# Interleaving the first normalisation's projections with the fold of the edge sums in a two-layer graph network kernel

## The chip, the cores and the metric

One core of a Trainium2 chip runs the whole kernel. The metric is device time in microseconds (us), the median of three runs. Engines are named as in the profile: PE (TensorE; PEld are its weight loads), DVE (VectorE), ACT (ScalarE), POOL (GpSimd), and SP, which issues DMAs.

## The reference

12500 nodes with 64 features, 400000 edges sorted by target, 64 features per edge. Two graph layers, each followed by a residual and a normalisation over the 64 features:

```python
def _L0_gnn_ref(x, src, dst, W_fc, b_fc, W_res, b_res):
    agg = segment_sum(x[src], dst, n)
    deg = segment_sum(ones_like(dst), dst, n)
    mean = agg / maximum(deg, 1.0)[:, None]
    h = relu(concatenate([x, mean], axis=-1) @ W_fc + b_fc)
    return h + x @ W_res + b_res

def _general_conv(x, edge_attr, src, dst, Wm, bm, We, be, Ws, bs):
    msg = x[src] @ Wm + bm + edge_attr @ We + be
    return segment_sum(msg, dst, n) + x @ Ws + bs

x = _layernorm(x + _L0_gnn_ref(x, ...))
x = _layernorm(x + conv2(relu(conv1(x))))      # both use edge_attr
```

## The kernel before, in words

The nodes lie in 98 blocks of 128 (`BLOCKS`). There are three rounds (`for r in range(3)`), and each adds up the rows of neighbours for one layer. Round 0 also builds a matrix of edge counts, and after its own sums it walks over all edge features: 728 edge steps (`ESTEPS`), eight at a time in a loop (`EB`), in which DVE marks targets (L931), ACT widens the marks (L1440), PE multiplies (L1196, one of eight PSUM banks per step) and DVE adds a finished bank to `sums_e` (L944; the last six banks, L955). `sums_e` lies over the whole of `abuf`, the buffer of the counts. SP loads the edge features (L1561), eight steps ahead.

Each block of `sums_e` holds two halves that must be added and turned. That is the fold: PE multiplies every block by `twofold`, two identities on top of each other (L1205, 98 blocks in 13 groups of up to 8, `FOLDS`, PSUM banks 0 to 3), and ACT copies each group into `easf`, which lies in `early` (L1445, counted by `e_out`).

Then comes the first normalisation, in 14 iterations of 7 blocks (`NITER`, `NB`):

- SP loads a piece of x, turned (L1525, 224 KB, two buffers `turned_a`, whose last row is set to one at L737).
- PE multiplies its 7 blocks by `w_in`, which holds `W_fc` and `W_res` with the biases in a 65th row (L1086, banks 4 and 5 or 6 and 7; `a_prod`). Iteration i waits until DVE has read the banks of iteration i-2 (`a_relu`). A float32 product shows as two instructions, so 7 blocks are 14 rows.
- POOL scales the neighbour sums by `rdeg`, the reciprocal of the degree (L1257).
- DVE adds (L743), takes the relu and adds the residual (L745), sums the squares of the iteration before (L749, which waits for ACT's squares, L1363), sums for the mean (L752) and subtracts it (L754). A square root on ACT (L1365) and a reciprocal on DVE (L757) follow the last iteration.

A second loop of 14 iterations then scales (L768), turns (L1047) and projects (L1104) the rows for round 1.

All buffers of the normalisation lie in `abuf`, over `sums_e`. So every engine waits for `round_done`, which DVE raises (L960) when the last group of the fold is copied. `rdeg` is computed just before that (L957, L958). The order of all engines is written by hand; each engine runs its own program in order and meets the others through semaphores, and SP's DMAs go out in the order of its program.

## Time and profile before

| | |
|---|---|
| median of three runs | 3532.28 us (3532.06 to 3535.52) |
| profiled execution: its time | 3533.11 us |
| profiled execution: its span, first to last instruction | 3531.3 us |
| busy share of the span | PE 88%, PEld 81%, DVE 68%, POOL 60%, ACT 45% |
| mean granted TensorE clock | 0.963 of full speed |
| last add of the edge sums (L955) starts | 1979.78 us |
| fold on PE (L1205) | 1980.12 to 2002.2 us |
| projections on PE (L1086) | 2006.22 to 2052.6 us |
| reciprocal after the first normalisation (L757) starts | 2058.09 us |

The page has a share of busy time for the whole span, but the change touches 80 us of it, from the last edge steps near 1975 us to the second loop at 2059 us. So what matters is read from views of that stretch: the chain of waits, the table by stretches with the granted clock, and the groups of instructions.

### The profile page before, as it was taken

The numbers are of one execution on the slowest core, as the hardware profiler recorded it, in microseconds if no ns is written. First come the engines' busy times: TensorE is split into PE (matmuls) and PEld (weight loads), VectorE is DVE, ScalarE is ACT, GpSimd is POOL, SyncE is SP. The second block draws the span as 40 slices with busy tenths as digits, with TensorE's granted clock in tenths as the row PEclk, the third lists the DMA queues.
The fourth block names the chain that finished last, engine by engine and source line by source line (L and its number), as shares of the span: only waits on it lengthen the run. The fifth ranks groups of instructions, "written<-read, shape, count | busy, mean of one in ns | idle before, by whom it ended". The sixth has DMA issues, their size and how long they took to land.

```text
span 3531.3 us, 114817 instructions
## 1 busy us (share of the span) xinstructions
PE 3093.6 (88%) x38568; PEld 2874.1 (81%) x38568; DVE 2388.2 (68%) x6286; ACT 1585.1 (45%) x2164; POOL 2120.9 (60%) x2436
## 2 busy tenths in 40 slices
PE   0128999999999999899999979999999889999995
PEld 0127988888888888788888879999999789999995
DVE  8679998888888888799999673333333433333335
ACT  0122677778999999789999550000000400000000
POOL 5771345455666666544444257777777777777774
PEclk9859999999999999999999879999999999999998
DMA  3521455556666666678888439999999499999995
GB/s 87 144 19 44 163 196 208 202 211 229 239 244 243 244 242 243 233 229 253 253 253 252 119 139 384 393 396 381 400 384 384 172 363 394 393 387 398 386 388 222
DMA packets 234014, 928.09 MB, mean 263 GB/s; under 512 B 46723, under 2 KB 146193, under 8 KB 178030
## 3 DMA queue, kind: packets, MB, share of 16 engines
q1 hardware_dynamic: 182405, 844.73, 63.8%
q0 software_dynamic: 51392, 80.97, 7.9%
q10 hardware_dynamic: 154, 1.60, 0.2%
q8 instruction: 34, 0.56, 0.1%
q14 instruction: 29, 0.24, 0.0%
HBM read 676.56 MB, written 250.56 MB: 263 GB/s over the span
## 4 chain that ended last, share of the span: by engine, by line
PE 40%; POOL 19%; issue 17%; DVE 14%; DMA 5%; DVEq 5%; ACT 1%; ACTq 0%; POOLq 0%; SPq 0%
PE ps L1126 27%; POOL msg L1288 13%; PE ps L1149 8%; DVE union L816 5%; DMA msg<-y_tab,idx 3%; POOL abuf L1230 3%; DVE union L931 3%; PE ps L1118 3%; DVE abuf L944 3%; DVEq L944 2%; DVEq L471 2%; POOL union L1230 1%; PE ps L1086 1%; DMA abuf<-in_x_dram 1%; PE ps L1205 1%
## 5 line engine op out<-in xcount | busy, mean ns | idle before, releaser
L1288 POOL DMA_INDIRECT msg<-y_tab,idx x1512 | 1611.3, 1066 | 922.2 <-issue 469.6
L1126 PE MATMUL ps<-union,abuf 128*128 128x192 bf16 x14112 | 1206.4, 248 | 14.9 <-DVEq L787 10.2
L1126 PEld LDWEIGHTS ps<-union,abuf 128*128 128x128 f16 x14112 | 1173.6, 99 | 17.9 <-issue 10.6
L1418 ACT ACTIVATE abuf<-ps 128x784 f16<-128x784 f32 x1152 | 949.1, 824 | 261.4 <-PE ps L1149 236.6
L816 DVE TENSOR_TENSOR union<-lane,union 128x1568 f16<-128x1568 f16 (+1 forms) x1384 | 911.7, 710 | 8.5 <-PE ps L1149 4.6
L1126 PE MATMUL ps<-early,abuf 128*128 128x195 bf16 x7154 | 809.3, 249 | 0.0
L1126 PEld LDWEIGHTS ps<-early,abuf 128*128 128x128 f16 x7154 | 641.9, 99 | 92.1
L1149 PE MATMUL ps<-union 128*128 128x98 f16 (+2 forms) x4192 | 661.8, 287 | 56.7 <-DVE union L816 55.5
L1394 ACT ACTIVATE idx<-src_g 128x7 int32 (+1 forms) x216 | 44.4, 205 | 1257.1 <-PE ps L1118 1237.9
L808 DVE TENSOR_TENSOR acc<-acc,ps 128x64 f32 (+1 forms) x1015 | 225.0, 222 | 412.4 <-DVE acc L808 239.3
L1196 PE MATMUL ps<-union 128*64 128x128 f32 x7280 | 458.7, 278 | 24.0 <-ACT union L1440 19.6
L1196 PEld LDWEIGHTS ps<-union 128*64 128x64 f32 x7280 | 395.5, 137 | 87.4 <-DVE abuf L944 74.3
L1440 ACT ACTIVATE union<-union 128x1280 f32<-128x1280 f16 x364 | 443.5, 1268 | 35.8 <-DVE union L931 35.3
L1149 PEld LDWEIGHTS ps<-union 128*128 128x128 f16 x4192 | 353.7, 108 | 98.5 <-issue 59.3
L1308 POOL TENSOR_TENSOR rel_e<-early,base_e 128x10 f16 x728 | 226.1, 330 | 247.4 <-DVE union L931 244.5
L931 DVE TENSOR_TENSOR union<-lane,rel_e 128x640 f16<-128x640 f16 x728 | 352.2, 484 | 4.4 <-POOL rel_e L1308 1.4
L895 DVE TENSOR_REDUCE part_d<-ps 128x64 f32<-128x192 f32 x144 | 51.6, 358 | 353.1 <-PE ps L1126 353.1
L794 DVE TENSOR_SCALAR hot_g<-lane,codes 128x128 f16<-128x128 f16 x1008 | 184.2, 269 | 63.9 <-DVE acc L808 62.2
L1118 PE MATMUL ps<-msg,hot_g 128*128 128x64 bf16 (+1 forms) x4536 | 181.7, 195 | 45.8 <-DMA msg<-y_tab,idx 45.3
L944 DVE TENSOR_TENSOR abuf<-abuf,ps 128x128 f32 x728 | 204.9, 281 | 15.8 <-issue 7.2
L1118 PEld LDWEIGHTS ps<-msg,hot_g 128*128 128x128 f16 x4536 | 169.1, 99 | 54.4 <-DMA msg<-y_tab,idx 53.8
L865 DVE TENSOR_TENSOR acc<-acc,ps 128x65 f32 x504 | 110.0, 218 | 69.0 <-DVE acc L865 53.8
(229 smaller groups left out, 1342.2 us busy)
## 6 DMA issues: line engine op xcount, KB each, us to landing
abuf<-a_dram SPq DMA_DIRECT2D x288, 1568.0 KB
a_dram<-abuf SPq DMA_DIRECT2D x72, 3136.0 KB
union<-in_edge_attr_dram SPq DMA_DIRECT2D x728, 160.0 KB, 3.1
msg<-y_tab,idx POOLq DMA_INDIRECT x1512
y_tab<-union SPq DMA_DIRECT2D x28, 336.0 KB, 2.2
abuf<-in_x_dram SPq DMA_DIRECT2D x28, 224.0 KB, 3.5
y_tab<-early SPq DMA_DIRECT2D x7, 682.5 KB, 5.2
out_dram<-union SPq DMA_DIRECT2D x2, 800.0 KB, 3.5
```

Source lines behind the costliest of these rows:

```text
L808: V.tensor_tensor(to, to, tile_ps(r, j, k).unsqueeze(1), ALU.add).then_inc(s_add[r], 1)
L816: return V.tensor_tensor(to.rearrange("p s (c u) -> p s c u", u=2), lanes.unsqueeze(1).to_broadcast([P, n, width // 2, 2]), codes[:, which ...
L931: marks = V.tensor_tensor(mark_e[:, h, :, :].rearrange("p j (c u) -> p j c u", u=2), lane16[:, 0:P].rearrange("p (c u) -> p c u", u=2).uns ...
L944: V.tensor_tensor(to, to, ps[:, b, 0:P], ALU.add).then_inc(e_add, 1)
L1118: last = nc.tensor.matmul(tile_ps(r, j, k), hot_g[:, s, :], msg[:, s, c * width_of[r]:(c + 1) * width_of[r]], start=c == 0, stop=c == 2)
L1126: last = nc.tensor.matmul(ps[:, bank, 0:3 * width_of[r]], abuf[:, buffer, hi * P:(hi + 1) * P], ycols[r][:, hi, :], start=hi == 0, stop=hi ...
L1149: nc.tensor.matmul(ps[:, w % 4, 0:WIN].rearrange("p (h d) -> p h d", d=WD)[:, :, d0:d0 + wd], hot_c[:, n, WIN:WIN + P], hot_c[:, n, 0:HIS ...
L1196: last = nc.tensor.matmul(ps[half:half + D, h, 0:P], feats[:, h, j * D:(j + 1) * D], hot_e[:, h, j, :], start=j < 2, stop=j >= EG - 2)
L1288: pool.indirect_dma_start(msg[:, s, 0:3 * width_of[r]], None, y_tab[r], bass.IndirectOffsetOnAxis(ap=idx[:, s:s + 1], axis=0)).then_inc(ga ...
L1308: nc.gpsimd.tensor_tensor(rel_e[:, h, :, :], flat(dst_e[:, bass.ds(grp[h], 1), :]).unsqueeze(2) .to_broadcast([P, EG, 2]), base_e[:, bass. ...
L1418: A.activation(abuf[:, j, :].rearrange("p (h w d) -> p w h d", w=WPB, d=WD) [:, w:w + 2, :, :], ps[:, w % 4:w % 4 + 2, 0:WIN].rearrange("p ...
L1440: A.activation(hot_e[:, h:h + 2, :, :], mark_e[:, h:h + 2, :, :], ACT.Copy)\
```

## The change

The fold and the projections become one sequence on PE: projections 0 and 1, then by turns a group of the fold and a projection, each projection two ahead of the group. To make that possible, the normalisation's buffers leave `abuf`: `turned_a` goes to `early`, behind the fold's output, and `scaled_a`, `sum_a` and `square_a` go to the end of `union`, behind the buffers of the edge steps. `rdeg` and the rows of ones are made before the edge steps. SP loads x as soon as its last edge load is issued. POOL scales without waiting for `round_done`. ACT copies a group of the fold ahead of each square. `round_done` is raised after the reciprocal, ahead of the second loop.

```diff
@@ buffers
-        turned_a = norm_tile(XT, F1)
-        scaled_a, sum_a, square_a = (per_block(norm_tile(U)) for _ in range(3))
+        turned_a = [early[0:F1, BLOCKS * D + k * XT:BLOCKS * D + (k + 1) * XT] for k in range(2)]
+        BEHIND = EB * EG * (D + P // 2 + P)
+        scaled_a, sum_a, square_a = (per_block([union[:, BEHIND + (2 * n + k) * U:BEHIND + (2 * n + k + 1) * U]
+                                                for k in range(2)]) for n in range(3))
@@ DVE
-                    for t in turned_a:
-                        V.memset(t[D:F1, :], 1.0).then_inc(s_ones, 1)
...
                     dve.wait_ge(a_rstd, 1)
+                    dve.wait_ge(e_out, FOLDS)
+                    dve.sem_inc(round_done, 1)
...
+                for t in turned_a:
+                    V.memset(t[D:F1, :], 1.0).then_inc(s_ones, 1)
+                step(V.tensor_scalar(rdeg[:, :], acc[:, :, D], 1.0, None, ALU.max))
+                step(V.reciprocal(rdeg[:, :], rdeg[:, :]), "rdeg")
                 dve.wait_ge(s_pc, 1 + 2 * BC + BE)
...
-                dve.wait_ge(e_add, ESTEPS + LAG + EB)
-                step(V.tensor_scalar(rdeg[:, :], acc[:, :, D], 1.0, None, ALU.max))
-                step(V.reciprocal(rdeg[:, :], rdeg[:, :]))
-                dve.wait_ge(e_out, FOLDS)
-                dve.sem_inc(round_done, 1)
@@ PE
-                if r == 1:
-                    for i in range(NITER):
-                        pe.wait_ge(n_in[i % 2], 16 * (i // 2 + 1))
...
+                    def project(i):
+                        pe.wait_ge(n_in[i % 2], 16 * (i // 2 + 1))
+                        if i >= 2:
+                            pe.wait_ge(a_relu, i - 1)
+                        for b in range(NB):
+                            last = nc.tensor.matmul(both(i % 2, b), turned_a[i % 2][:, b * P:(b + 1) * P],
+                                                    w_in[:, :, :].rearrange("f c d -> f (c d)"), start=True, stop=True)
+                        last.then_inc(a_prod, 1)
+
+                    pe.wait_ge(s_ones, 2)
+                    pe.wait_ge(e_add, ESTEPS + 6 - (EB - LAG) + EB)
+                    project(0)
                     pe.wait_ge(e_add, ESTEPS + LAG + EB)
-                    for n in range(FOLDS):
...
+                    project(1)
+                    for n in range(NITER):
+                        if n < FOLDS:
+                            if n >= 4:
+                                pe.wait_ge(e_out, n - 3)
+                            for c in range(min(FB, BLOCKS - n * FB)):
+                                last = nc.tensor.matmul(ps[:, n % 4, c * D:(c + 1) * D], sums_e[:, n * FB + c, :],
+                                                        twofold[:, :], start=True, stop=True)
+                            last.then_inc(e_fold, 1)
+                        if n + 2 < NITER:
+                            project(n + 2)
@@ POOL
-                if r:
-                    pool.wait_ge(round_done, r + 1)
                 if r == 1:
+                    pool.wait_ge(s_v, mark["rdeg"])
                     for i in range(NITER):
...
+                if r:
+                    pool.wait_ge(round_done, r + 1)
@@ ACT
                     for i in range(NITER):
+                        if i < FOLDS:
+                            act.wait_ge(e_fold, i + 1)
+                            width = min(FB, BLOCKS - i * FB) * D
+                            A.activation(easf[:, i * FB * D:i * FB * D + width], ps[:, i % 4, 0:width], ACT.Copy)\
+                                .then_inc(e_out, 1)
                         act.wait_ge(a_mid, i + 1)
...
                     A.activation(rstd, root, ACT.Sqrt, bias=epst[:, :], scale=1.0 / D).then_inc(a_root, 1)
+                    act.wait_ge(round_done, r + 1)
...
-                    for n in range(FOLDS):
-                        act.wait_ge(e_fold, n + 1)
...
@@ SP
-                if r:
-                    sp.wait_ge(round_done, r + 1)
-                else:
+                if r == 0:
                     sp.wait_ge(s_v, mark["prepared"])
...
                         sp.dma_start(turned_a[i % 2][0:D, :], x[:, i * XT:(i + 1) * XT]).then_inc(n_in[i % 2], 16)
+                if r:
+                    sp.wait_ge(round_done, r + 1)
```

PE's program behind the loop of edge steps, before (L1196 edge steps, L1205 fold, L1086 projections, L1047 the second loop's turning; a float32 product counts once here):

```order
L1196 MATMUL ps<-union 64x128 x5
L1189 REGISTER_ALU
L1189 COMPARE_AND_BRANCH
L1205 MATMUL ps<-twofold,abuf 128x64 x98
L1086 MATMUL ps<-w_in,abuf 128x128 x98
L1047 MATMUL ps<-ident,abuf 128x128 x14
```

and now (L1186 edge steps, L1195 projections, L1209 fold):

```order
L1186 MATMUL ps<-union 64x128 x5
L1179 REGISTER_ALU
L1179 COMPARE_AND_BRANCH
L1195 MATMUL ps<-w_in,early 128x128 x14
L1209 MATMUL ps<-twofold,abuf 128x64 x8
L1195 MATMUL ps<-w_in,early 128x128 x7
L1209 MATMUL ps<-twofold,abuf 128x64 x8
L1195 MATMUL ps<-w_in,early 128x128 x7
```

Two projections lead, and from then on each group of 8 blocks of the fold is followed by one projection of 7 blocks; all 98 and 98 blocks are still there.

ACT's program in the same place, before (L1440 edge steps, L1445 copies of the fold, L1363 squares):

```order
L1440 ACTIVATE union<-union 128x1280 x4
L1435 REGISTER_ALU
L1435 COMPARE_AND_BRANCH
L1445 ACTIVATE early<-ps 128x512 x12
L1445 ACTIVATE early<-ps 128x128
L1363 ACTIVATE abuf<-acc 128x448 x14
L1365 ACT_TABLE_LOAD
```

and now (L1370 copies, L1375 squares):

```order
L1453 ACTIVATE union<-union 128x1280 x4
L1448 REGISTER_ALU
L1448 COMPARE_AND_BRANCH
L1370 ACTIVATE early<-ps 128x512
L1375 ACTIVATE union<-acc 128x448
L1370 ACTIVATE early<-ps 128x512
L1375 ACTIVATE union<-acc 128x448
```

The square of iteration i, for which DVE's next iteration waits, now stands behind the copy of fold group i.

## Rows read from the trace of the kernel before

**Rows 1.** Chain of waits, edge steps to second loop (start us, us, what).

```profile
1979.78 0.30 DVE abuf L955
1980.12 21.67 PE ps L1205 x192
...
2002.65 3.44 DMA abuf<-in_x_dram
2006.22 3.34 PE ps L1086 x14
2009.58 3.25 DMA abuf<-in_x_dram
...
2049.76 0.63 DVE abuf L743
...
2052.77 0.63 DVE abuf L743
```

**Rows 2.** Table by stretches (stretch, length, busy by engine, PEclk, DMA share, GB/s).

```profile
core 0: us, PE busy (x) PEld busy (x) DVE busy (x) ACT busy (x) POOL busy (x), PEclk, DMA share, GB/s
1980.10:2002.20 22.10, 22.08 (x196) 21.96 (x196) 1.01 (x2) 6.96 (x12) 0.00 (x0) 1.00 0.01 1
2002.20:2006.20 4.00, 0.02 (x1) 0.01 (x1) 1.61 (x2) 0.38 (x2) 1.83 (x2) 0.89 0.44 115
2006.20:2012.50 6.30, 6.28 (x28) 6.04 (x28) 2.49 (x4) 0.16 (x1) 0.94 (x1) 0.50 0.14 36
2006.20:2052.60 46.40, 45.11 (x196) 42.63 (x196) 37.34 (x64) 6.92 (x12) 15.58 (x16) 0.50 0.21 60
...
2059.50:2062.90 3.40, 3.33 (x16) 3.33 (x17) 0.61 (x3) 1.54 (x3) 0.00 (x0) 0.50 0.92 295
2064.00:2068.00 4.00, 3.97 (x37) 3.78 (x36) 2.06 (x4) 3.71 (x9) 1.39 (x2) 1.00 0.11 44
```

**Rows 3.** Timeline of PEld (start us, us, engine, line, operation, count).

```profile
2019.47 3.06 PEld L1086 LDWEIGHTS ps<-w_in,abuf 65*128 65x128 f32 x14 [0.56 <-DMA abuf<-in_x_dram]
2059.57 2.85 PEld L1047 LDWEIGHTS ps<-ident,abuf 128*128 128x128 f32 x14 [7.20 <-DVE abuf L768]
...
2073.73 0.75 PEld L1047 LDWEIGHTS ps<-ident,abuf 128*128 128x128 f32 x7 [0.53 <-DVE abuf L768]
2074.45 1.64 PEld L1104 LDWEIGHTS ps<-w_cat,abuf 128*128 128x128 f32 x14
```

**Rows 4.** Timeline of the hand-over from edge steps to fold.

```profile
1971.72 2.55 SPq L1561 DMA_DIRECT2D union<-in_edge_attr_dram  x4
1977.58 1.08 PEld L1196 LDWEIGHTS ps<-union 128*64 128x64 f32 x20 [0.26 <-issue]
1978.56 0.29 DVE L955 TENSOR_TENSOR abuf<-abuf,ps 128x128 f32 x1 [0.26 <-DVE abuf L955]
```

**Rows 5.** Groups of instructions from 1980 to 2059 us.

```profile
L1257 POOL TENSOR_TENSOR abuf<-acc,rdeg 128x448 f32<-128x448 f32 x14 | 13.1, 937 | 63.1 <-DVE abuf L743 32.0 <-DVEq L960 31.0
L743 DVE TENSOR_TENSOR abuf<-abuf,ps 128x448 f32<-128x448 f32 x14 | 8.7, 620 | 9.7 <-PE ps L1086 9.6
L1363 ACT ACTIVATE abuf<-acc 128x448 f32<-128x448 f32 x14 | 8.1, 577 | 45.7 <-DVE acc L754 45.7
L1445 ACT ACTIVATE early<-ps 128x512 f32<-128x512 f32 (+1 forms) x13 | 7.3, 572 | 17.9 <-PE ps L1205 17.9
L737 DVE MEMSET abuf<- 1x896 f32 x2 | 1.6, 805 | 21.9 <-ACT early L1445 21.8
L958 DVE RECIPROCAL rdeg<-rdeg 128x98 f32<-128x98 f32 x1 | 0.8, 766 | 0.0
```

**Rows 6.** DMA issues from 1980 to 2059 us (KB each, median us to landing).

```profile
abuf<-in_x_dram SPq DMA_DIRECT2D x14, 224.0 KB, 3.3
```

**Rows 7.** Timeline ahead of the edge steps.

```profile
1492.88 5.33 POOL L1302 MEMSET abuf<- 128x6272 f32 x1 [19.16 <-DVEq L913]
1498.07 0.23 DVE L918 TENSOR_TENSOR twofold<-ident 128x64 f32<-128x64 f32 x1 [7.47 <-ACT early L1339]
```

More of the change, by code:

```diff
@@ L326, in gnn_program @@
         bias_b = per_block(norm_tile(U))
-        turned_a = norm_tile(XT, F1)
         assert used[0] <= HIS * P // 2
-        used[0] = 0
-        scaled_a, sum_a, square_a = (per_block(norm_tile(U)) for _ in range(3))
-        assert used[0] <= HIS * P // 4
+        turned_a = [early[0:F1, BLOCKS * D + k * XT:BLOCKS * D + (k + 1) * XT] for k in range(2)]
+        BEHIND = EB * EG * (D + P // 2 + P)
+        scaled_a, sum_a, square_a = (per_block([union[:, BEHIND + (2 * n + k) * U:BEHIND + (2 * n + k + 1) * U]
+                                                for k in range(2)]) for n in range(3))
+        assert BLOCKS * D + 2 * XT <= YW0 and EG * GROUPS <= BLOCKS * D and BEHIND + 6 * U <= UNION
+        assert FOLDS <= NITER
         regs = smallf[:, 11 * CG:11 * CG + 64]
@@ L1076, in _ @@
                     pe.wait_ge(round_done, r + 1)
-                    pe.wait_ge(s_ones, 2 * min(r, 1))
                 pe.wait_ge(s_v, mark["prepared"])
-                if r == 1:
-                    for i in range(NITER):
-                        pe.wait_ge(n_in[i % 2], 16 * (i // 2 + 1))
-                        if i >= 2:
-                            pe.wait_ge(a_relu, i - 1)
-                        for b in range(NB):
-                            last = nc.tensor.matmul(both(i % 2, b), turned_a[i % 2][:, b * P:(b + 1) * P],
-                                                    w_in[:, :, :].rearrange("f c d -> f (c d)"), start=True, stop=True)
-                        last.then_inc(a_prod, 1)
                 for i in range(NITER + 1) if r else ():
@@ L1198, in _ @@
                             last.then_inc(e_mm[h], 1)
-                    pe.wait_ge(e_add, ESTEPS + LAG + EB)
-                    for n in range(FOLDS):
-                        if n >= 4:
-                            pe.wait_ge(e_out, n - 3)
-                        for c in range(min(FB, BLOCKS - n * FB)):
-                            last = nc.tensor.matmul(ps[:, n % 4, c * D:(c + 1) * D], sums_e[:, n * FB + c, :], twofold[:, :],
-                                                    start=True, stop=True)
-                        last.then_inc(e_fold, 1)
+                    def project(i):
[9 more added lines that the diff above has]
+                    project(0)
+                    pe.wait_ge(e_add, ESTEPS + LAG + EB)
+                    project(1)
[9 more added lines that the diff above has]
+                            project(n + 2)
         @block.gpsimd
@@ L1352, in _ @@
             for r in range(3):
-                if r:
+                if r == 2:
                     act.wait_ge(round_done, r + 1)
-                else:
+                elif r == 0:
                     act.wait_ge(s_v, mark["prepared"])
@@ L1441, in _ @@
                                 .then_inc(e_hot[h // 2], 1)
-                    for n in range(FOLDS):
-                        act.wait_ge(e_fold, n + 1)
-                        width = min(FB, BLOCKS - n * FB) * D
-                        A.activation(easf[:, n * FB * D:n * FB * D + width], ps[:, n % 4, 0:width], ACT.Copy)\
-                            .then_inc(e_out, 1)
             squares = union[:, 0:BLOCKS * D].rearrange("p (b d) -> p b d", d=D)
@@ L1515, in _ @@
             for r in range(3):
-                if r:
-                    sp.wait_ge(round_done, r + 1)
-                else:
+                if r == 0:
                     sp.wait_ge(s_v, mark["prepared"])
```

## The prediction

> **What bounds the kernel now.** I read the chain of waits first, where the last link of each step stands. From the last add of the edge sums to the second loop it is one thread: the fold on PE (21.67 us), a wait for x (3.44), and then by turns a pair of projections on PE (about 3.35 us a projection) and a wait of about 3.3 us for the next piece of x, up to DVE's last two iterations, which start at 2049.76 and 2052.77 [rows 1]. Nothing runs beside the fold but ACT's copies.
>
> Then I read the table by stretches, for the clock. Here the reader is to see something that the busy shares hide: PE is granted 1.00 (2.4 GHz) all through the fold; it idles while x is on its way, and the clock has fallen by 2006.2; and the projections then run at 0.50 (1.2 GHz) for 46 us, although PE is busy in 45.1 of 46.4 us [rows 2]. So the projections are slow for two reasons: a 3.3 us load that two buffers do not hide, and half the clock. Third, the timeline of weight loads gives the price of the same work at both levels: 14 loads of a projection (7 blocks) take 3.06 us at half clock; the second loop's projections, as many columns but 128 rows instead of 65, take 1.64 us for 14 at full clock [rows 3].
>
> **The change, part by part.**
>
> *Where PE starts.* The fold waits for the last add of the edge sums; projection 0 needs only the banks 4 and 5, whose adds are done with the fourth of the six last ones, 1978.56 + 0.29 = 1978.85. PE's last edge step issues its loads until 1978.66 [rows 4]. So projection 0 starts at about 1978.95, and the wait for the last add (1980.07) ends inside it. For this x must be there. SP is done with the edge loads at 1971.72 + 2.55 = 1974.27 [rows 4], and x took 3.44 us the first time, two loads together, and 3.3 after that [rows 1, 6]: it lands near 1978, with no edge load behind it on the queue. 0.9 us of slack; if it is late, PE waits that much once.
>
> *The sequence on PE.* 14 projections and 12 full groups of the fold stand ahead of the end of projection 13 (the thirteenth group, 2 blocks, comes after it). A group is 16 of the 196 instructions that took 22.1 us, 1.80 us [rows 2], 12 of them 21.6. For a projection I have two ends: 3.06 us at half clock and 1.64 at full [rows 3]. I take 1.64, 14 of them 22.96, because the fold alone held 1.00 for 22 us [rows 2], the edge steps ahead of it run at full clock too, and PE now goes from the one to the other without the idle stretch in which the clock fell. PE ends projection 13 at 1978.95 + 22.96 + 21.6 = 2023.5.
>
> *No new wait inside it.* Projection i+2 needs its x, issued when projection i ends; between them lie two groups and a projection, 1.80 + 1.64 + 1.80 = 5.24 us, against 3.3 us to landing [rows 6]. Only projection 2 has less, 1.64 + 1.80 = 3.44 us; the load of x is about 0.1 us faster. The relu of iteration i, for which projection i+2 waits, comes 1.3 us after DVE starts on it and has as much room. POOL's scaling (0.94 us each [rows 5]) starts as soon as POOL's part of the edge steps ends and is never last.
>
> *DVE and ACT.* DVE needs 3.01 us an iteration (2049.76 to 2052.77 [rows 1]), less than PE's 1.64 + 1.80 = 3.44. But ACT now copies fold group i ahead of square i, and DVE's iteration i+1 waits for that square. From the end of projection i+1: the group 1.80, copy 0.57, square 0.58 [rows 5], then DVE's last three operations, 3.01 less two of 0.62 and their gaps, 1.74, and some 0.15 of hand-overs: 4.84 us. That is 1.4 us after the next projection ends. It does not add up over iterations, since neither the group nor the projection waits for this end, only for the relu in front of it. So DVE starts its last iteration 1.4 us behind PE, at 2024.9. Before, it started at 2052.77. What follows (the last iteration, the root, the reciprocal) is the same work: **27.9 us gained**.
>
> *What is moved.* The rows of ones (1.6 us) and the reciprocal of the degrees (0.77 and a shorter operation [rows 5]) go ahead of the edge steps, into 7.47 us in which DVE waited for ACT's copies of the targets [rows 7]: nothing, while that cover is there; without it 2.6 us. POOL clears half of `sums_e` beside them, as before, until 1498.2, right behind that cover.
>
> *Behind the loop.* `round_done` now comes after the reciprocal, and behind it ACT's first copy of the second loop, POOL's biases and SP's loads. ACT's copy ran 0.9 us earlier before, but PE also needs DVE's scaled rows, which end as late; POOL's first bias is due some 7 us after. I take nothing, at most 0.1. PE idles some 7 us ahead of the second loop, as before (2052.6 to 2059.57), and starts it at half clock in both. There, 14 loads take 2.85 us where 7 take 0.75 at full [rows 3]: between a start at full clock and as long again at half, 1.35 us either way. I take nothing.
>
> *Sum.* 3533.11 us is the profiled execution, 0.83 above the median of 3532.28; against the latter **3504.4 us**. A run of this kernel tells a change from none at about 0.2%, 7 us.
>
> **A rule against the rows.** The clock fell while PE idled, and did not come back under projections that kept PE busy; other work did bring it back: the second loop starts at 0.50 and has 1.00 from 2064 [rows 2]. The Trainium skill (TensorE: Matmul & The Clock Gate, section "Why this matters for your kernels") says that matmuls keep the fast clock as long as PE does not idle between bursts. By that rule the new sequence stays at full clock and 3504.4 stands; by the same rule the projections of before should have risen, and the row says 0.50, so here page and measurement differ, and the measurement decides. The trace has no projection at full clock. That leaves rivals 1 and 2.
>
> **The rivals.**
>
> 1. *The projections pull the clock down, and the fold with it: slower.* For it: 46 us of them at 0.50 with PE busy [rows 2]. Against it: they were never at full clock to begin with, and half the time now goes to work that held it. Price: a weight load of 128 rows took 2.85/14 at half and 0.75/7 at full, 1.90 times as long [rows 3], so a group 3.42 us; 1978.95 + 14 x 3.06 + 12 x 3.42 = 2062.8, DVE 0.2 behind: 10.2 us later than before, 3542.5 us. It is slower than before from a group of 2.57 us on.
> 2. *Half clock in the projections, full in the fold*, or half in part of the stretch: 1978.95 + 14 x 3.06 + 12 x 1.80 = 2043.4, DVE 0.2 behind, 9.2 us gained: 3523.1.
> 3. *The chain over ACT sets the pace.* Should the 4.84 us (group, copy, square, DVE's end) come in series, because PE falls behind DVE after all, DVE's last iteration starts at 1980.8 + 13 x 4.84 = 2043.7: 3523.2. Against it: PE waits for the relu alone.
> 4. *x comes late every time.* If it takes 6.6 us, twice the 3.3 [rows 6], two projections go by in 6.6 + 1.64 us, 4.12 instead of 3.44 each, 8.2 us over 12: 3512.6. Against it: the DMA queues carry nothing else there.
> 5. *The order on PE is not what sets the end*, say because ACT's copies hold the banks: no change. The chain speaks against it.
>
> **How the numbers follow.** Forecast 0.76, rival 1 0.08, rival 2 0.07, rivals 3 and 4 0.04 each, rival 5 0.01. The forecast's own ends: 1.4 us less if DVE keeps up, 1.35 less if the second loop starts at full clock, some 0.8 less if projections of 65 rows go a little faster than 1.64; the other way the same, and 2.6 if the moved operations are not covered: 3500 to 3511. To hold 8 in 10 the range goes on to rivals 2 to 4: 3500 to 3524. Faster by over 0.2% is the forecast and rivals 2 to 4, 0.90; within 0.2% 0.02; slower, rival 1, 0.08.
>
> **What would show it.** In the table by stretches of the changed kernel: PEclk 1.00 from 1979 to 2023, where 0.50 in any part of it is rival 1 or 2. In the chain: PE's projections and fold by turns without a DMA between them, and DVE's last iteration at 2024.9. In the timeline: 14 weight loads of a projection in 1.64 us, groups of 1.80, projection 0 at 1979. In the groups: DVE's L749 waiting for ACT's square, some 0.4 us each time. DVE's moved operations between 1490.6 and 1493.5 with L918's counterpart where it was. Wrong is the forecast if a projection takes 3 us, if PE waits for x, or if the stretch up to the edge steps grows.

## The result, and the profile after

The changed kernel takes 3510.43 us (median of 4 runs, 3509.63 to 3512.45) against 3533.90 us for the kernel before in the same comparison (4 runs, 3532.06 to 3536.56). The ratio is 0.9934, with a 95% interval of 0.9918 to 0.9949: 23.5 us faster, where 27.9 were forecast. The profiled run took 3509.63 us with a span of 3507.9 us, and the mean granted clock of the whole span went from 0.963 to 0.970.

The stage itself went as forecast. The chain of waits of the changed kernel, from the first projection on (start us, us, what; L1195 projections, L1209 fold, L743 the first operation of an iteration on DVE, its last start the last iteration):

```profile
1985.37 1.81 PE ps L1195 x14
1987.18 0.02 issue
1987.20 3.27 DMA early<-in_x_dram
1990.47 0.04 issue
1990.51 1.83 PE ps L1195 x14
1992.34 1.73 PE ps L1209 x16
1994.07 1.62 PE ps L1195 x14
...
2025.84 1.75 PE ps L1209 x16
...
2028.11 0.58 ACT union L1375
2028.71 0.62 DVE small L749
...
2030.43 0.62 DVE union L743
```

Before, the chain passed through a DMA between the projections [rows 1]. Now x is on the chain only once, and from 1990.5 on a projection (1.62 us) and a group of the fold (1.73) follow each other without a gap. The last link is the one over ACT that the prediction named: copy, square, DVE's sum of squares. The table by stretches shows why a projection takes 1.62 us:

```profile
core 0: us, PE busy (x) PEld busy (x) DVE busy (x) ACT busy (x) POOL busy (x), PEclk, DMA share, GB/s
1986.50:2027.60 41.10, 41.05 (x368) 40.91 (x368) 35.08 (x60) 11.68 (x22) 11.23 (x12) 1.00 0.25 68
```

PE is busy in 41.05 of 41.10 us, and the clock is 1.00 (2.4 GHz) in all of them, where the projections ran at 0.50 before [rows 2]. The weight loads, the wait of the prediction's projection 2 (0.18 us) and DVE's wait for the square, in the timeline and in the groups:

```profile
1985.34 3.20 PEld L1195 LDWEIGHTS ps<-w_in,early 65*128 65x128 f32 x28 [0.30 <-issue]
1988.46 1.87 PEld L1209 LDWEIGHTS ps<-twofold,abuf 128*128 128x128 f32 x16
1990.51 1.64 PEld L1195 LDWEIGHTS ps<-w_in,early 65*128 65x128 f32 x14 [0.18 <-DMA early<-in_x_dram]
```

```profile
L749 DVE TENSOR_REDUCE small<-union 128x7 f32<-128x448 f32 x14 | 8.7, 620 | 5.4 <-ACT union L1375 5.4
```

14 loads of 65 rows take 1.64 us [rows 3 have 3.06 at half clock], and a pair of projection and group 1.62 + 1.73 = 3.35 us in the chain. DVE's last iteration starts at 2030.43, 44.2 us after the last add of the edge sums (1986.20). Before it was 2052.77 less 1979.78, 73.0 us [rows 1]. So the stage gave **28.8 us**.

But the last add itself came at 1986.20 instead of 1979.78: **6.4 us of the gain were lost ahead of the stage**, in work that the prediction put down at nothing. Three points of the trace divide it: up to the start of the conversion of the edge targets (L886, before L884) the run was 1.05 us shorter; from there to the first marking of targets it took 14.1 us instead of 12.7; and from the first to the last of the 728 markings 480.1 instead of 474.1. Three sets of rows tell where. First the timeline ahead of the edge steps of the changed kernel:

```profile
1492.23 5.33 POOL L1309 MEMSET abuf<- 128x6272 f32 x1 [19.55 <-DVEq L915]
1492.47 1.75 DVE L920 MEMSET early<- 1x896 f32 x2 [2.93 <-issue]
1494.25 3.37 DVE L921 TENSOR_SCALAR rdeg<-acc 128x98 f32<-128x98 f32 x1
1497.66 0.77 DVE L922 RECIPROCAL rdeg<-rdeg 128x98 f32<-128x98 f32 x1
1498.46 0.22 DVE L924 TENSOR_TENSOR twofold<-ident 128x64 f32<-128x64 f32 x1
```

The shorter operation of `rdeg` (L921) takes 3.37 us, where it took 0.25 behind the loop in the kernel before. It ends at 1497.62, just after POOL's clearing of `sums_e` ends (1492.23 + 5.33 = 1497.56). The rows of ones (L920), beside the same clearing, take what they took, 0.805 us each [rows 5]. In all five traces with this order (the changed kernel twice, and three of the experiments below) L921 takes 3.36 or 3.37 us and ends 0.06 or 0.07 us after the clearing. The Trainium skill (SBUF — State Buffer, section "Who interferes with whom") says that a DVE `tensor_scalar` may use the ports that DVE shares with GpSimd, and that whichever of the two starts second is blocked until the other ends; the trace agrees, 3.37 us beside POOL and 0.25 without it.

Second, the end of the edge loop (L937 marks targets, L1262 is POOL's scaling):

```profile
1976.81 2.08 POOL L1262 TENSOR_TENSOR union<-acc,rdeg 128x448 f32<-128x448 f32 x2
1976.82 1.27 DVE L937 TENSOR_TENSOR union<-lane,rel_e 128x640 f16<-128x640 f16 x1
...
1978.21 1.02 DVE L937 TENSOR_TENSOR union<-lane,rel_e 128x640 f16<-128x640 f16 x1
...
1979.36 0.48 DVE L937 TENSOR_TENSOR union<-lane,rel_e 128x640 f16<-128x640 f16 x1
```

POOL's first two scalings no longer wait for the fold, so they run while DVE still marks, and two markings take 1.27 and 1.02 us instead of 0.48. From the 721st marking to the last it is 5.80 us in all five traces in which POOL scales this early, and 4.56 or 4.57 in the nine others: 1.24 us lost. The same section says that a DVE operation with both inputs in SBUF contends with a GpSimd operation that reads SBUF; a marking (`lane` and `rel_e`) is one, and the rows agree.

Third, the middle of the edge loop, where nothing was changed. The stretch from 1520 to 1960 us in both kernels, markings alone (L931 before, L937 now):

```profile
1520.00:1960.00 440.00, 328.27 (x679) 1.00 0.84 253
```

```profile
1520.00:1960.00 440.00, 325.83 (x671) 1.00 0.84 250
```

679 markings in 440 us before, 671 now, at the same clock. 32 steps, one turn of the loop, take 21.0 us instead of 20.75: from the 65th marking to the 721st it is 430.7 us instead of 425.6, 5.1 of the 6.0. A distance between two markings is 0.60 us, and 0.72 to 0.75 at every fourth (0.99 at the jump back), where DVE loads four block numbers into registers, which the trace doesn't count as busy. In the changed kernel two of the eight such places, the one 4 and the one 24 steps behind the jump back, take 0.87 and 0.86 us. DVE's program in front of the loop has become longer by the four moved operations.

### The profile page after: what moved, and what is told of

The parts are those of the page before. It is cut to its first block, busy times and chain, and to the rows that moved or that the text cites. A ratio compares the mean times of both kernels' runs of the same rounds, so it can differ in the third digit from the quotient of the medians.

```text
span 3507.9 us, 114818 instructions
## 1 busy us (share of the span) xinstructions
PE 3071.3 (88%) x38568; PEld 2853.7 (81%) x38568; DVE 2393.0 (68%) x6286; ACT 1584.9 (45%) x2164; POOL 2121.4 (60%) x2436
## 4 chain that ended last, share of the span: by engine, by line
PE 44%; POOL 17%; issue 15%; DVE 14%; DMA 5%; DVEq 5%; ACT 0%; ACTq 0%; POOLq 0%; SPq 0%
PE ps L1116 31%; POOL msg L1295 11%; PE ps L1139 8%; DVE union L818 5%; DMA msg<-y_tab,idx 4%; DVE union L937 3%; POOL abuf L1236 3%; PE ps L1108 3%; DVE abuf L950 2%; DVEq L950 2%; DVEq L473 2%; POOL union L1236 1%; PE ps L1195 1%; PE ps L1209 1%; POOL abuf L1279 0%
## 5 line engine op out<-in xcount | busy, mean ns | idle before, releaser
L1116 PE MATMUL ps<-union,abuf 128*128 128x192 bf16 x14112 | 1204.9, 248 | 12.4 <-DVEq L789 10.2
L1407 ACT ACTIVATE idx<-src_g 128x7 int32 (+1 forms) x216 | 44.4, 206 | 1256.3 <-PE ps L1108 1254.0
L1186 PE MATMUL ps<-union 128*64 128x128 f32 x7280 | 459.8, 278 | 30.4 <-ACT union L1453 25.6
L1186 PEld LDWEIGHTS ps<-union 128*64 128x64 f32 x7280 | 395.3, 137 | 95.0 <-DVE abuf L950 81.5
L937 DVE TENSOR_TENSOR union<-lane,rel_e 128x640 f16<-128x640 f16 x728 | 355.3, 488 | 4.6 <-POOL rel_e L1315 1.4
```

Source lines behind the costliest of these rows:

```text
L937: marks = V.tensor_tensor(mark_e[:, h, :, :].rearrange("p j (c u) -> p j c u", u=2), lane16[:, 0:P].rearrange("p (c u) -> p c u", u=2).uns ...
L1116: last = nc.tensor.matmul(ps[:, bank, 0:3 * width_of[r]], abuf[:, buffer, hi * P:(hi + 1) * P], ycols[r][:, hi, :], start=hi == 0, stop=hi ...
L1186: last = nc.tensor.matmul(ps[half:half + D, h, 0:P], feats[:, h, j * D:(j + 1) * D], hot_e[:, h, j, :], start=j < 2, stop=j >= EG - 2)
```

## The experiments

Two questions stood open. **Where do the 6.4 us come from?** Theory: from the moved DVE and POOL operations, in the three ways above; rival: from the spread between runs. **What makes the stage shorter?** Theory: that PE never stands still, so that the clock stays up, and that this takes the turns; rivals: x early is enough, or the fold can hold or restore the clock by itself.

### Repeats of both kernels

The kernel before, and the changed one.

> The kernel before, once more, for the spread of its edge loop. Theory A (the 4 us by which the edge loop grew in the changed kernel, between 1520 and 1970 us, are spread between executions): the loop from the first to the last marking on DVE differs from the 474.1 us of the first trace by 2 us or more. Theory B (the change makes the loop slower through the place or address of something): 474 us again, within 1 us.

> The changed kernel, once more. Theory A: first to last marking on DVE differs from 480.1 us by 2 us or more. Theory B: 480 us again, within 1 us. Either way the granted clock stays at 1.00 from the first projection to the last, and DVE's first operation on the degrees (a tensor_scalar over 98 elements) again takes over 3 us beside POOL's clearing.

Before: 3531.98 us, conversion to first marking 13.7 us, first to last marking 473.8. Changed: 3508.97 us, 14.5 and 479.5. The loop's length repeats within 0.6 us in either kernel, so its 6 us are no spread. The 1.45 us at the start are less sure: 12.7 and 13.7 before, 14.1 and 14.5 now.

### POOL scales only after the last markings

```diff
                 if r == 1:
                     pool.wait_ge(s_v, mark["rdeg"])
+                    pool.wait_ge(e_mark[EB // 2 - 1], ESTEPS // EB + 1)
```

> POOL starts to scale only when the last marks of the edge steps are made. Theory: POOL's two scalings beside the last edge steps held up DVE's markings there (1.27 and 1.02 us instead of 0.48, and two stalls of 0.6 us), so the last markings take 0.48 us again and the last add comes 2 to 2.5 us earlier, relative to the edge step 8 before the end; projections start as much earlier, since 0.95 us of scaling still fit beside projection 0. Rival: the stalls there come from instruction loading or the DMA of x and stay; then no change, or up to 1 us slower because DVE waits for POOL at its first iteration.

All 728 markings of this kernel (columns: min, median and longest ns, first and last start):

```profile
L937 DVE TENSOR_TENSOR union<-lane,rel_e x728: 474/483/548, 1504.9 to 1982.9; 128x640 f16<-128x640 f16 x182
```

The longest marking is 0.548 us instead of 1.27, and the loop takes 478.1 us instead of 480.1 and 479.5. What POOL's early scaling costs on DVE is read at the end of the loop, 4.56 us instead of 5.80: 1.2 us, less than the 2 to 2.5 that I expected. The rest of the difference (0.2 and 0.8 us) lies ahead of it in the loop, whose length differs by 0.6 us between the two runs of the changed kernel. The last iteration starts nearly as long after the last add as in the changed kernel (44.4 us, 44.2 there), so POOL has the time. The whole kernel, 3512.02 us in its single run, doesn't show it: 1.2 us are within what runs differ by.

### The reciprocal behind the clearing

```diff
-                step(V.tensor_scalar(rdeg[:, :], acc[:, :, D], 1.0, None, ALU.max))
-                step(V.reciprocal(rdeg[:, :], rdeg[:, :]), "rdeg")
                 dve.wait_ge(s_pc, 1 + 2 * BC + BE)
...
                 step(V.memset(ps[:, EB - LAG:EB, 0:P], 0.0), "zeros_e")
+                step(V.tensor_scalar(rdeg[:, :], acc[:, :, D], 1.0, None, ALU.max))
+                step(V.reciprocal(rdeg[:, :], rdeg[:, :]), "rdeg")
```

> The reciprocal of the degrees is made after the clearing of the last banks, when POOL's clearing is over and DVE waits 1.4 us for POOL's first targets anyway. Theory: the tensor_scalar took 3.37 us because POOL was clearing; here it takes 0.25 us, and the distance from the end of DVE's conversion of targets to the first marking shrinks from 12.3 us to about 10.9, as in the kernel before: 1.4 us faster. Rival: the operation is slow for its operand (a column with a stride of 65 elements); then it takes 3 us here too and the first marking comes 2 us later.

Timeline of the same place:

```profile
1495.61 5.33 POOL L1309 MEMSET abuf<- 128x6272 f32 x1 [19.55 <-DVEq L915]
...
1502.66 0.25 DVE L928 TENSOR_SCALAR rdeg<-acc 128x98 f32<-128x98 f32 x1
1502.95 0.77 DVE L929 RECIPROCAL rdeg<-rdeg 128x98 f32<-128x98 f32 x1
```

The same operation takes 0.25 us once POOL's clearing has ended, and the first marking comes 12.9 us after the conversion instead of 14.1. 1.2 us of the 1.45 would be regained there, by one trace. Over all traces, the five with the reciprocal beside the clearing have 13.7 to 14.5 us in this place, 14.15 on the mean, and the nine others 12.7 to 13.7, 13.06 on the mean: 1.1 us, with ends that touch. The total of the single run (3513.21 us) doesn't show it either: its stretch up to the conversion was 3.4 us longer than in the profile of the changed kernel.

### Four instructions more in DVE's program

Before the loop, four clearings of one element each, into a place that is not read after them. First in the kernel before:

```diff
+                for k in range(4):
+                    V.memset(part_d[0:1, 1, k:k + 1], 0.0)
                 dve.wait_ge(s_pc, 1 + 2 * BC + BE)
```

> The kernel before with four tiny clearings (one element each) on DVE where the change puts its four moved operations, and nothing else. Theory (the edge loop of the changed kernel is slower because DVE's program lies four instructions further on, so that two of its eight loads of block numbers in 32 steps take 0.13 us longer): 32 steps go from 20.75 to about 21.0 us, first to last marking from 474 to 478 or more, and the kernel is 4 to 6 us slower than before, with the longer steps at the same two places behind the jump back (5th and 25th step). Rival (another part of the change does it: the x loads, POOL's scaling, the addresses of the buffers): 474 us, no change.

The markings of the same 440 us:

```profile
1520.00:1960.00 440.00, 324.58 (x671) 1.00 0.84 250
```

671, as in the changed kernel, with 21.00 us a turn and the longer distances at the same two places (0.87 and 0.85). Loop and data are those of the kernel before, so four instructions ahead of the loop are enough. First to last marking: 478.9 us, 4.8 more than in the profile of before. The kernel also had something that I did not expect: it took 3557.13 us, 26 more than before beside it. Some 18 of these are the fold, nearly all of which ran at half clock: the last iteration starts 90.7 us after the last add instead of 73.0. That is taken up below.

Then the changed kernel with both edits of the two sections above and the four clearings, eight instructions further than before:

> The changed kernel with POOL's scaling behind the last marks, the reciprocal of the degrees behind the clearing of the banks, and four tiny clearings on DVE ahead of the edge steps, so that DVE's program lies four instructions further on again. Theory of the place of the program: the sum of 32 steps is another than 21.0 us, 20.75 if the two loads of block numbers are lucky again; then first to last marking 472 to 474 us. Rival: the loop takes what it took, 478 us, wherever the program lies. By either, the last markings take 0.48 us, and the tensor_scalar on the degrees 0.25.

Here my expectation missed. The longest marking is 0.544 us, the start takes 13.1 us, as meant. But a turn of the loop still takes 21.0 us, slow at the same two places (479.1 first to last marking; 3510.34 us in all), so four more do not bring the old pace back. What the runs show is that the pace depends on what stands ahead of the loop: from the 65th to the 721st marking all ten traces with four or eight instructions more have 430.2 to 430.7 us, and the four with the program of before 425.6 or 425.7. The pattern by which it does is open.

### DVE's program as before

The decisive version: DVE's program ahead of the loop is again that of before. POOL makes the rows of ones, and DVE computes `rdeg` behind the last add. The rest of the change stays.

```diff
@@ DVE
-                for t in turned_a:
-                    V.memset(t[D:F1, :], 1.0).then_inc(s_ones, 1)
-                step(V.tensor_scalar(rdeg[:, :], acc[:, :, D], 1.0, None, ALU.max))
-                step(V.reciprocal(rdeg[:, :], rdeg[:, :]), "rdeg")
...
                     V.tensor_tensor(to, to, ps[:, EB - LAG + k, 0:P], ALU.add).then_inc(e_add, 1)
+                step(V.tensor_scalar(rdeg[:, :], acc[:, :, D], 1.0, None, ALU.max))
+                step(V.reciprocal(rdeg[:, :], rdeg[:, :]), "rdeg")
@@ POOL
+                    pool.wait_ge(s_v, mark["dst_e"])
+                    for t in turned_a:
+                        pool.memset(t[D:F1, :], 1.0).then_inc(s_ones, 1)
+                    pool.wait_ge(s_ones, 2)
                     pool.wait_ge(round_done, 1)
```

> The changed kernel with the rows of ones made by POOL, right behind DVE's conversion of the targets, and the reciprocal of the degrees behind the last add of the edge sums, as in the kernel before. DVE's program ahead of its edge loop is then that of the kernel before, and POOL cannot scale beside the last marks. Theory: 32 steps take 20.75 us again and first to last marking 474 us instead of 480; conversion to first marking 12.6 to 13.1 us instead of 14.1; DVE's first iteration starts 2.3 us after the start of the last add instead of 1.1, which PE does not wait for, so that the last iteration still starts 44.2 us after it. Some 7 us faster than the changed kernel, 3503 us. Rival: the loop's pace hangs on something else in the change; then 478 us, and 3508.

Its markings in the 440 us:

```profile
1520.00:1960.00 440.00, 328.24 (x679) 1.00 0.84 253
```

679 again. All three losses are gone: 12.8 us to the first marking, 472.9 from the first to the last, no long marking. The last add starts at 1978.5, and DVE's last iteration 44.2 us later. The time is 3503.01 us (4 runs, 3500.44 to 3507.01), ratio to before 0.9916, interval 0.9901 to 0.9931. Against before it gains 28.5 us where the change gained 23.5. The two were not run side by side and the intervals of their ratios overlap, but no run of this version (at most 3507.01) reaches one of the changed kernel (at least 3508.97 in the five seen). Its price is that DVE's first iteration waits 1.1 us for POOL's first scaling, which now follows `rdeg`.

### ACT takes the square ahead of the copy

In the version above, the square of iteration i goes ahead of the copy of fold group i, so that the chain over ACT gets shorter by one copy.

```diff
                     for i in range(NITER):
+                        act.wait_ge(a_mid, i + 1)
+                        if i >= 2:
+                            act.wait_ge(a_var, i - 1)
+                        A.activation(square_a[i % 2], feat[:, blocks_of(i), :], ACT.Square).then_inc(a_sq, 1)
                         if i < FOLDS:
                             act.wait_ge(e_fold, i + 1)
...
-                        act.wait_ge(a_mid, i + 1)
-                        if i >= 2:
-                            act.wait_ge(a_var, i - 1)
-                        A.activation(square_a[i % 2], feat[:, blocks_of(i), :], ACT.Square).then_inc(a_sq, 1)
```

> As the last one, and ACT takes square i ahead of fold group i's copy. Theory: DVE no longer waits 0.36 us for the square in each iteration and is no longer 1.4 us behind PE at the end; the last iteration starts 42.8 us after the last add instead of 44.2: 1.4 us faster, 3501.5 us. Rival: the copy now comes later, and PE waits for its bank; then the pairs on PE take longer than 3.35 us.

DVE now waits for PE instead of ACT, 0.36 us in each of the last iterations:

```profile
L743 DVE TENSOR_TENSOR union<-union,ps 128x448 f32<-128x448 f32 x14 | 8.7, 619 | 3.9 <-PE ps L1193 2.8 <-POOL union L1260 1.1
L749 DVE TENSOR_REDUCE small<-union 128x7 f32<-128x448 f32 x14 | 8.6, 612 | 0.6 <-ACT union L1372 0.6
```

The last iteration starts 43.16 us after the last add instead of 44.25: the lag of DVE behind PE was there, 1.1 us of it, and is gone. In the total it can't be told from nothing: 3503.76 us (5 runs, 3500.53 to 3505.18), interval of the ratio 0.9905 to 0.9932.

### The fold whole, and not by turns

The changed kernel, but behind projections 0 and 1 PE runs the whole fold, and then projections 2 to 13. ACT copies all groups before the first square.

```diff
@@ PE
-                    for n in range(NITER):
-                        if n < FOLDS:
...
-                        if n + 2 < NITER:
-                            project(n + 2)
+                    for n in range(FOLDS):
...
+                    for n in range(2, NITER):
+                        project(n)
```

> The changed kernel, but PE does projections 0 and 1, then the whole fold, then projections 2 to 13 in a row; ACT copies the whole fold ahead of the squares. It keeps the early loads of x and the buffers, so it tells the interleaving from the rest. Theory 1 (the clock falls only where PE idles for long, and projections keep it): 1.00 throughout, DVE sets the pace with 3.0 us an iteration, and its last iteration starts about 59.5 us after the last add of the edge sums, against 44.2 in the changed kernel: 15 us slower than that. Theory 2 (projections of 65 rows with short gaps let the clock fall, the fold between them holds it up): 1.00 in the fold, 0.50 from some point in the row of projections, 3.06 us each, the last iteration some 64 us after the last add: 20 us slower, only 3 us better than before.

Table by stretches and chain of waits:

```profile
1990.00:2010.00 20.00, 20.00 (x182) 20.00 (x181) 2.42 (x5) 6.13 (x11) 1.32 (x2) 1.00 0.08 23
2016.00:2020.00 4.00, 3.06 (x14) 3.07 (x15) 3.90 (x8) 0.58 (x1) 1.18 (x2) 0.54 0.21 57
2020.00:2050.00 30.00, 28.69 (x128) 27.25 (x126) 26.52 (x46) 5.19 (x9) 7.48 (x8) 0.50 0.22 62
```

```profile
2012.04 1.63 PE ps L1195 x14
2013.67 0.02 issue
2013.69 3.20 DMA early<-in_x_dram
2016.89 0.04 issue
2016.93 3.37 PE ps L1195 x14
```

The fold and two projections behind it run at full clock (1.63 us). Then PE waits for x, 1.72 us without work, and from there on projections take 3.37 us at 0.50 until the end, with a wait for x of 0.2 to 0.4 us ahead of every second one. DVE's last iteration starts 62.6 us after the last add instead of 44.2, between the 59.5 and the 64 that I expected: of the 28.8 us that the stage gave, 18.4 are lost, and the run takes 3531.77 us (before, beside it, 3530.72). So early x and other buffers alone are worth some 10 us of the 28.8; the rest came with the turns, which hide x behind a group of the fold and so keep PE from standing still. Two things are not shown: whether more buffers for x would do the same behind a whole fold, and whether a row of projections without any wait would hold the clock.

### x late

The changed kernel, with SP's first load of x held back until the last add:

```diff
                 if r == 1:
+                    sp.wait_ge(e_add, ESTEPS + LAG + EB)
                     for i in range(NITER):
```

> The changed kernel, but SP loads the first x only after the last add of the edge sums. PE then idles some 4.5 us ahead of projection 0, and the clock falls. It shows what the interleaved sequence does from half clock. Theory 1 (the fold's groups bring the clock back, as 128-row work did in the second loop): 0.50 for a few us, then 1.00; the kernel is 4.5 + 3 to 6 us slower than the changed one. Theory 2 (the mixture cannot bring it back, as the projections alone could not): 0.50 to the end of the sequence, a projection 3.06 and a group about 3.4 us, PE 6.5 us per pair; 4.5 + some 40 us slower, slower than the kernel before by 20 us.

Timeline of PE and of the weight loads, then the table:

```profile
1992.78 6.13 PE L1195 MATMUL ps<-w_in,early 65*128 65x128 f32 x28 [4.75 <-DMA early<-in_x_dram]
```

```profile
2062.49 3.53 PEld L1209 LDWEIGHTS ps<-twofold,abuf 128*128 128x128 f32 x16
2065.91 3.11 PEld L1195 LDWEIGHTS ps<-w_in,early 65*128 65x128 f32 x14
```

```profile
1988.00:1994.00 6.00, 1.25 (x8) 1.25 (x7) 0.59 (x3) 0.00 (x0) 0.00 (x0) 0.92 0.29 76
...
2020.00:2068.00 48.00, 48.00 (x226) 48.00 (x226) 21.73 (x37) 8.48 (x16) 6.55 (x7) 0.50 0.12 36
```

One wait of 4.75 us ahead of the sequence, and the whole sequence runs at 0.50, although PE is busy in all of 48 us. The last iteration starts 86.9 us after the last add instead of 44.2, and the run takes 3556.39 us. In the stage that is 13.9 us more than before (73.0), 4.75 of them the wait; without it 9.1, close to the 10.2 of the prediction's rival 1, but reached from another cause: the mixture doesn't pull the clock down (the changed kernel), and here it doesn't bring it back either. The whole kernel is 25.7 us above before, beside it, because the work ahead of the stage is slower too, the edge loop alone by 5.7 us (479.8 instead of 474.1).

### What the fold does to the clock by itself

The run with four clearings had the fold of the kernel before at half clock. A second run of the same kernel, timed:

> The kernel before with the four tiny clearings, once more and timed. Theory (whether the clock falls ahead of the fold hangs on where the 1.2 us in which PE waits for the last adds fall, and once it has fallen the fold does not bring it back): executions of two kinds, some near 3536 us with the fold at 1.00 in 22 us, some near 3557 with the fold at 0.50 in 40 us. Rival (the place of DVE's program costs the clock every time): all near 3557 us. In both, 32 edge steps take 21.0 us.

3556.09 us (4 runs, 3553.97 to 3558.74), ratio 1.0067, interval 1.0051 to 1.0082. The expectation of two kinds of executions missed: all five runs have a long time and a mean clock of 0.956 or 0.957, and the two that were traced have the fold at 0.50. The timeline and the table of the first of them:

```profile
1987.20 7.06 PE L1207 MATMUL ps<-twofold,abuf 128*128 128x64 f32 x42 [1.26 <-DVE abuf L957]
```

```profile
1987.00:1989.00 2.00, 1.80 (x16) 1.80 (x17) 1.16 (x3) 0.00 (x0) 0.00 (x0) 1.00 0.03 8
1989.00:1991.00 2.00, 2.00 (x14) 2.00 (x14) 0.00 (x0) 0.60 (x1) 0.00 (x0) 0.65 0.00 0
1995.00:2027.00 32.00, 32.00 (x151) 31.92 (x150) 0.00 (x0) 5.97 (x10) 0.00 (x0) 0.50 0.00 1
```

Ahead of the fold PE stands still for 1.26 us, from its last edge step to the last add. The fold starts at 1.00, falls, and stays at 0.50 though PE has no gap. The kernel before has the same stop (1.23 us, and 1.26 in its repeat), and there the fold keeps 1.00 and takes 22.1 us. The repeat:

```profile
1982.00 22.10 PE L1205 MATMUL ps<-twofold,abuf 128*128 128x64 f32 x196 [1.26 <-DVE abuf L955]
```

So the stop can't be the whole cause. The theory was that without it the clock doesn't fall. To test this, PE fills it with six products whose results are not used, as soon as bank 0 is free:

```diff
+                    pe.wait_ge(e_add, ESTEPS + EB)
+                    for c in range(6):
+                        nc.tensor.matmul(ps[:, 0, c * D:(c + 1) * D], ident[:, :], twofold[:, :], start=True, stop=True)
                     pe.wait_ge(e_add, ESTEPS + LAG + EB)
```

> The kernel before with the four tiny clearings, and six products of 128 rows by 64 columns (of the fold's own form, on the identity, into a bank that the fold overwrites) on PE in the 1.26 us in which it waits for the last adds ahead of the fold. Their results are not used. Theory (the clock falls in the fold because PE stands still ahead of it): the fold stays at 1.00, its 196 instructions take 22 us, the last iteration's start comes 73 us after the last add as in the kernel before, and the kernel takes some 3536 us, 5 above the kernel before for the slower edge loop. Rival (it is not the gap: the fold itself, or what the edge steps do ahead of it, lets the clock fall): the fold at 0.50, 40 us, the kernel at 3556 us again.

```profile
1983.75 2.02 PE L1198 MATMUL ps<-union 128*64 128x128 f32 x30
1985.70 1.55 PE L1204 MATMUL ps<-twofold,ident 128*128 128x64 f32 x12
1987.09 7.09 PE L1210 MATMUL ps<-twofold,abuf 128*128 128x64 f32 x62
```

```profile
1991.00:2009.00 18.00, 18.00 (x163) 18.00 (x162) 0.00 (x0) 6.10 (x11) 0.00 (x0) 1.00 0.00 1
```

The fold is back at 1.00, and the time at 3538.25 us (10 runs, 3536.80 to 3540.16): 17.8 us less than the kernel without the six products. The reported ratio of 1.0013 (0.9995 to 1.0031) hides what remains, because 2 of the 13 runs of the kernel before, 3553.09 and 3550.25, were some 20 us longer than its other 11 (3527.56 to 3532.56). Against its median, 3530.19, this kernel is 8.1 us slower, of which the slower edge loop accounts for some 5. No trace was taken of the two long runs. Their mean clock was 0.955 and 0.956, that of the other eleven 0.962 to 0.966 and that of the program with four clearings 0.956, so that half clock in the fold fits them in time and clock; where it fell isn't shown. Why one program falls in all its runs and the other in few, with the same stop, is open.

## Why the prediction was right, and where it was wrong

The sign, the mechanism and the range held (3510.43 within 3500 to 3524); the 3504.4 us were 6.0 too low, 1.6 of them because the kernel before measured 3533.90 in this comparison and not the 3532.28 from which the forecast was taken. In gain it is 23.5 us for 27.9. Two of the prediction's own signs of being wrong showed, both small: PE waited for x once (0.18 us), and the first marking came 0.4 us later than before (1501.84 and 1501.44) although the run was 1.05 us ahead at the conversion. Step by step:

- **Where PE starts.** Right: projection 0 starts 0.83 us ahead of the last add (1985.37 and 1986.20), just as in the prediction (1978.95 and 1979.78), and x was there.
- **The sequence.** Right on the choice between full and half clock, which was the largest open term: 1.62 us a projection. A pair took 3.35 us instead of 3.44, and PE's end of projection 13 came some 43.9 us after its start instead of 44.6.
- **No new wait.** Nearly: projection 2, the one with 3.44 us of room, waited 0.18 us for x.
- **DVE and ACT.** Right: DVE waited for the square each time (5.4 us in 13 waits), without adding up. Its last iteration starts 45.1 us after PE's start, forecast 45.95. With the square first the lag is gone, 1.1 us where 1.4 were forecast, and the total doesn't show it.
- **What is moved: "nothing, while that cover is there".** This step failed, and with the next one it is more than the whole of the miss: 7.5 us, against 0.9 more than forecast in the stage and 2.1 from stretches that the change doesn't touch. The prediction priced the three operations by their durations (1.6, 0.77 and a shorter one) against a wait of 7.47 us [rows 7]. It saw POOL's clearing in the same rows, but not that it would hold one of them. Nor is all of the wait to be had: DVE reaches the moved work at 1492.47 only, behind 2.93 us in which it waits, further up in its program, for the counts to be stored (`stored`). With 0.25 turned into 3.37 us, what is left is not long enough: 1.1 to 1.5 us are lost. And it did not count that four more instructions ahead of a loop of 728 steps can change the loop's pace: 4.6 to 5.1 us, shown by the kernel before with nothing else added, and by its reversal.
- **"POOL's scaling ... is never last."** True of the scaling, but it asked only whether POOL would be late. The early scaling ran beside DVE's last markings and cost DVE 1.2 us.
- **Behind the loop.** Right: from DVE's last iteration to the end 1477.5 us, 1478.5 before.

Sum: 28.8 gained in the stage, 7.5 lost ahead of it (1.5 and 6.0), 1.05 and 1.0 gained by the run in stretches that the change doesn't touch: 23.4 of span. These last 2 us are luck: the stretch behind the loop differs by as much between runs of one kernel (1478.6 and 1475.4 us in the two profiles of before).

On the rule of the Trainium skill (TensorE: Matmul & The Clock Gate, section "Why this matters for your kernels") that the prediction weighed: that matmuls keep the fast clock while PE doesn't idle between bursts was borne out by the changed kernel (41.05 of 41.10 us busy, 1.00) and by the filled stop. That busy matmuls also regain it was not, in 48 us of the late-x run, as in the projections of before. Rival 1 was wrong as a cause and real as a danger: it came about through a stop of 4.75 us ahead of the sequence. Rival 4's place was right (x), and its 8.2 us for the waits alone may be too little: with the fold whole, the clock fell with the first wait for x. Late x inside the turns was not run.

## What to carry to other kernels

Work that has no gaps of its own should be placed between loads, so that the engine never waits: here a stop of 4.75 us ahead of the work cost 43 us with the wait itself, and one of 1.26 us cost some 18 in one program and nothing in the repeat of another, because the clock fell or didn't, and the work behind it did not raise it again. An operation moved under cover is free only if nothing that runs beside it there holds it up; look up which engine works beside it, and compare the duration with a row of the same operation beside the same neighbour. After moving anything ahead of a long loop, compare the loop's pace per turn in both traces before looking at the stage that was meant.

## What the runs showed of the hardware that was not expected

- Instructions placed ahead of a loop on DVE change its pace: 20.75 us a turn of 32 steps with the program of before, 21.0 with four instructions added (the changed kernel, and before with four clearings) and with eight, always longer at the same two places of the turn. The Trainium skill (Runtime: NRT & Kernel Launch, section "Instruction fetch mechanics") says that an engine's program is fetched in blocks and that a taken branch can stall the fetch; whether a boundary of such blocks lies behind this, no run here shows.
- A fold of 128x64 products holds 1.00 for 22 us [rows 2], and did so after a stop of 1.26 us in the repeat of before. In another program, after the same stop, it fell to 0.50 within 4 us of its start and stayed there for 32 us and more, in both traces (all five runs of it are as long); with the stop filled by products whose results are not used it stays at 1.00.
- POOL's operations lengthen DVE's: a clearing holds a `tensor_scalar` to its end (0.25 to 3.37 us) but not a clearing on DVE (0.805 us with and without it), and a product of two buffers on POOL lengthens a marking from 0.48 to 1.27 us.
